# The first query block and the last key block of a macaron attention: from three reduced 32-bit matmuls to one plain 32-bit matmul

## The reference

```python
x = x + 0.5 * ffn(layernorm(x))     # 16 experts of width 128, top 2, plus a shared part of width 512
x = x + attention(layernorm(x))
x = x + 0.5 * ffn(layernorm(x))     # the same weights again
```

```python
qkv = q @ w_qkv.T                                          # 4096 + 1024 + 1024 columns
scores = einsum('bskgd,btkd->bkgst', qh, kh) / sqrt(128)
scores = where(causal, scores, finfo.min)
probs = softmax(scores, axis=-1)
attn = einsum('bkgst,btkd->bskgd', probs, vh)
return attn.reshape(B, S, 4096) @ w_dense.T
```

## Time and profile before

| what | value |
|---|---|
| median of three executions | 1210.75 us |
| profiled execution | 1207.59 us, of which the span is 1205.9 us |
| TensorE matmul busy | 1130.7 us, 94% of the span |
| VectorE, ScalarE, GpSimd busy | 701.6, 557.6 and 473.4 us |
| TensorE's share of the chain that ended last | 86% |
| stretch from 250 to 960 us (attention) | TensorE busy 708.59 of 710 us |

### The profile page before, as it was taken

One profiled execution on the slowest core, in us unless ns is written; L12 is line 12 of the kernel. 1 busy time (PEld: TensorE's weight loads), 2 busy tenths in 40 slices (PEclk: granted clock), 3 DMA queues, 4 the chain that ended last, 5 costly groups with the idle time before them and its releaser, 6 DMA issues.

```text
span 1205.9 us, 20326 instructions
## 1 busy us (share of the span) xinstructions
PE 1130.7 (94%) x6110; PEld 943.2 (78%) x6111; DVE 701.6 (58%) x1836; ACT 557.6 (46%) x1352; POOL 473.4 (39%) x485
## 2 busy tenths in 40 slices
PE   5989996789999999999999999999999989989994
PEld 4777774678888888888888888888888876877773
DVE  5767776855455545454545454554554556867766
ACT  3336662346435445344544443534553543246650
POOL 1266556116315324323432532531532410365545
PEclk9999998889999999999999999999999999999998
DMA  9986547101101010010010110010100007744546
GB/s 356 346 303 212 161 148 244 53 1 36 53 2 36 9 44 0 35 52 0 35 52 0 35 52 0 35 52 0 35 1 1 1 15 287 301 141 157 160 144 209
DMA packets 38603, 114.62 MB, mean 95 GB/s; under 512 B 4384, under 2 KB 4384, under 8 KB 36512
## 3 DMA queue, kind: packets, MB, share of 16 engines
q1 hardware_dynamic: 33440, 97.30, 22.4%
q0 software_dynamic: 5120, 16.78, 4.1%
HBM read 79.20 MB, written 34.87 MB: 95 GB/s over the span
## 4 chain that ended last, share of the span: by engine, by line
PE 86%; DVE 4%; DMA 3%; issue 2%; ACT 2%; POOL 2%; DVEq 0%; SPq 0%; ACTq 0%; POOLq 0%
PE bank L1221 22%; PE bank L1286 15%; PE bank L1252 10%; PE bank L1298 10%; PE bank L1200 7%; PE bank L1127 6%; PE bank L1234 6%; PE bank L1208 4%; PE bank L1143 2%; POOL yg L484 2%; PE bank L1169 2%; PE bank L1188 1%; PE bank L1100 1%; DMA raw_w<-in_ffn_w 1%; PE bank L1088 1%
## 5 line engine op out<-in xcount | busy, mean ns | idle before, releaser
L498 POOL TENSOR_TENSOR scores<-scores,pinv 128x512 f32<-128x512 f32 (+3 forms) x256 | 176.7, 723 | 378.9 <-DVE pinv L996 378.9
L651 ACT ACTIVATE pT_hi<-bank 128x384 fp32r<-128x384 f32 (+1 forms) x192 | 93.9, 524 | 137.1 <-PE bank L1234 137.1
L450 POOL TENSOR_TENSOR tback_lo<-experts,tback_hi 128x768 fp32r<-128x768 f32 x62 | 115.0, 1857 | 74.4 <-ACT tback_hi L593 73.4
L676 ACT ACTIVATE oT_hi<-bank 128x512 fp32r<-128x512 f32 x64 | 38.3, 599 | 221.5 <-PE bank L1298 221.5
L664 ACT ACTIVATE scores<-scores,nmax 128x512 f32<-128x512 f32 (+3 forms) x256 | 140.3, 557 | 0.3 <-DVE nmax L986 0.3
L966 DVE TENSOR_TENSOR pT_lo<-bank,pT_hi 128x384 fp32r<-128x384 f32 (+1 forms) x192 | 109.5, 598 | 46.9 <-ACT pT_hi L651 46.8
L986 DVE CUSTOM_DVE_ANT_0 scores<-bank,causal 128x512 f32<-128x512 f32 (+3 forms) x256 | 112.2, 486 | 2.2 <-issue 0.2
L970 DVE TENSOR_TENSOR oT_lo<-bank,oT_hi 128x512 fp32r<-128x512 f32 x64 | 44.3, 692 | 112.7 <-ACT oT_hi L676 112.7
L1286 PE MATMUL bank<-wds_hi,oT_hi 128*128 128x512 f32 x256 | 105.5, 412 | 1.4 <-DVE oT_lo L970 1.4
L1221 PE MATMUL bank<-xnT_hi,wqs_hi 128*128 128x512 f32 x256 | 106.7, 417 | 0.0
L1221 PE MATMUL bank<-xnT_lo,wqs_hi 128*128 128x512 f32 x256 | 101.8, 398 | 0.0
(11 more groups left out here) (192 smaller groups left out, 2854.0 us busy)
## 6 DMA issues: line engine op xcount, KB each, us to landing
experts<-in_ffn_w SPq DMA_DIRECT2D x32, 768.0 KB, 10.1
xn<-x_rows SPq DMA_DIRECT2D x62, 256.0 KB, 2.7
y_rows<-xn SPq DMA_DIRECT2D x62, 256.0 KB, 2.0
raw_q<-in_wq SPq DMA_DIRECT2D x8, 1024.0 KB, 5.3
raw_d<-in_wd SPq DMA_DIRECT2D x8, 1024.0 KB, 4.8
x_rows<-experts SPq DMA_DIRECT2D x1, 7936.0 KB, 30.0
raw_w<-in_ffn_w SPq DMA_DIRECT2D x8, 768.0 KB, 7.6
raw_kv<-in_wkv SPq DMA_DIRECT2D x8, 512.0 KB, 3.3
```

Of the source, the lines that this page charges most:

```text
L450: nc.gpsimd.tensor_tensor(tback[par][1][:], experts[:, bass.ds(at + FRONT, GU - FRONT)], tback[par][0][:].bitcast(F32), ALU.subtract).then ...
L498: nc.gpsimd.tensor_tensor(s, s, pinv[k % 2][:, i:i + 1].to_broadcast([P, P * (i + 1)]), ALU.mult).then_inc(att.normed, 1)
L651: nc.scalar.activation(pT[0][:, lo_col:hi_col], bank[b][:, 0:hi_col - lo_col], ACT.Copy).then_inc(att.t_hi, 1)
```

## The change

Six plain 32-bit tiles of 128 by 128 are added. ScalarE copies into them, from the same PSUM banks as before: the first 128 queries (`q_first`), the first 128 keys (`k_first`, one for each of two buffers), the last 128 values (`v_last`, two buffers), and the last 128 columns of the transposed probabilities (`pT_last`). TensorE's product for query block 0 is now one matmul of `q_first` with `k_first`, and for key block 3 one matmul of `v_last` with `pT_last`. The halves of what these blocks read are no longer made for `qT` (384 columns in place of 512), `vv` (384) and the third part of `pT` (256 in place of 384). The halves of `kT` are made in full, since the other query blocks read its first 128 keys.

```diff
@@ turned_hi: the third part of pT, and the copies that ScalarE makes
+                    if n == 2:
+                        nc.scalar.activation(pT_last[:], bank[b][:, hi_col - lo_col:hi_col - lo_col + P], ACT.Copy)
                     nc.scalar.activation(pT[0][:, lo_col:hi_col], bank[b][:, 0:hi_col - lo_col],
                                          ACT.Copy).then_inc(att.t_hi, 1)
+
+                def query(src):
+                    nc.scalar.activation(q_first[:], src[:, 0:P], ACT.Copy)
+                    nc.scalar.activation(qT[0][:, P:], src[:, P:], ACT.Copy).then_inc(att.proj_hi, 1)
+
+                def key(b):
+                    nc.scalar.activation(k_first[b][:], bank[0][:, 0:P], ACT.Copy)
+                    nc.scalar.activation(kT[b][0][:], bank[0][:], ACT.Copy).then_inc(att.proj_hi, 1)
+
+                def value(b):
+                    nc.scalar.activation(v_last[b][:], bank[0][:, 3 * P:], ACT.Copy)
+                    nc.scalar.activation(vv[b][0][:, 0:3, :].rearrange("p c d -> p (c d)"), bank[0][:, 0:3 * P],
+                                         ACT.Copy).then_inc(att.proj_hi, 1)
@@ ScalarE's slot
-                        turned_hi(u - 1, 2, COL[2], TRI[ST], 6)
+                        turned_hi(u - 1, 2, COL[2], COL[3], 6)
-                        nc.scalar.activation(qT[0][:], bank[0][:], ACT.Copy).then_inc(att.proj_hi, 1)
+                        query(bank[0])
...
@@ VectorE's slot
-                        turned_lo(u - 1, 2, COL[2], TRI[ST], 6)
+                        turned_lo(u - 1, 2, COL[2], COL[3], 6)
-                        low(qT[1][:], bank[0][:], qT[0][:], att.proj_out)
+                        low(qT[1][:, P:], bank[0][:, P:], qT[0][:, P:], att.proj_out)
...
-                            low(vv[1 - b][1][:].rearrange("p c d -> p (c d)"), bank[0][:],
-                                vv[1 - b][0][:].rearrange("p c d -> p (c d)"), att.proj_out)
+                            low(vv[1 - b][1][:, 0:3, :].rearrange("p c d -> p (c d)"), bank[0][:, 0:3 * P],
+                                vv[1 - b][0][:, 0:3, :].rearrange("p c d -> p (c d)"), att.proj_out)
...
@@ TensorE's slot
                             for i, c in tiles:
+                                if i == 0:
+                                    last = nc.tensor.matmul(bank[bk][:, c:c + P], q_first[:], k_first[b][:],
+                                                            start=True, stop=True)
+                                    continue
                                 for m, (a, z) in enumerate(PARTS):
...
                         for j in range(ST):
                             if j != 3:
                                 pe.wait_ge(att.t_lo, 3 * (u - 1) + j + 1)
+                            if j == ST - 1:
+                                last = nc.tensor.matmul(bank[1][:, j * P:SEQ], v_last[bu][:], pT_last[:],
+                                                        start=False, stop=True, skip_group_check=True)
+                                continue
                             for m, (a, z) in enumerate(PARTS):
```

More of the change, by code:

```diff
@@ L162, in build @@
             causal = sb("causal", [P, 512], F32, st)
+            q_first = sb("q_first", [P, P], F32, st)
+            k_first = [sb(f"k_first{b}", [P, P], F32, st) for b in range(2)]
+            v_last = [sb(f"v_last{b}", [P, D], F32, st) for b in range(2)]
+            pT_last = sb("pT_last", [P, P], F32, st)
             nmax = [sb(f"nmax{p}", [P, ST], F32, st) for p in range(2)]
@@ L683, in slot @@
                         if r == 1:
[L684 removed]
+                            key(1 - b)
                         else:
[L686 to L687 removed]
+                            value(1 - b)
                     if k < 8:
@@ L698, in attention @@
                 turned_norm(1, 0)
-                for n, dst, b in ((1, kT[0][0][:], 0), (3, qT[0][:], 4),
-                                  (4, vv[0][0][:].rearrange("p c d -> p (c d)"), 0)):
-                    act.wait_ge(att.proj_mm, n)
-                    nc.scalar.activation(dst, bank[b][:], ACT.Copy).then_inc(att.proj_hi, 1)
+                act.wait_ge(att.proj_mm, 1)
+                key(0)
+                act.wait_ge(att.proj_mm, 3)
+                query(bank[4])
+                act.wait_ge(att.proj_mm, 4)
+                value(0)
                 att_slots(act, slot)
@@ L1033, in attention @@
                 dve.wait_ge(att.proj_hi, 2)
-                low(qT[1][:], bank[4][:], qT[0][:], att.proj_out)
+                low(qT[1][:, P:], bank[4][:, P:], qT[0][:, P:], att.proj_out)
                 dve.wait_ge(att.proj_hi, 3)
-                low(vv[0][1][:].rearrange("p c d -> p (c d)"), bank[0][:],
-                    vv[0][0][:].rearrange("p c d -> p (c d)"), att.proj_out)
+                low(vv[0][1][:, 0:3, :].rearrange("p c d -> p (c d)"), bank[0][:, 0:3 * P],
+                    vv[0][0][:, 0:3, :].rearrange("p c d -> p (c d)"), att.proj_out)
                 att_slots(dve, slot)
@@ L1299, in slot @@
                                                         pT[z][:, COL[j]:COL[j] + SEQ - j * P],
-                                                        start=(j == 0 and m == 0), stop=(j == ST - 1 and m == 2),
+                                                        start=(j == 0 and m == 0), stop=False,
                                                         skip_group_check=True)
```

3 lines of the change are left out of this document (removed).

## The result

| | before | changed |
|---|---|---|
| median, us (runs, lowest to highest) | 1209.16 (6, 1206.61 to 1211.13) | 1189.81 (6, 1187.85 to 1191.67) |
| profiled execution, us (span) | 1207.59 (1205.9) | 1191.12 (1189.4) |
| mean granted clock in it | 0.984 | 0.982 |

The changed kernel is faster: the ratio of the times is 0.9842 with the interval 0.9822 to 0.9861, 19.1 us by the ratio. Two more comparisons, each on a chip of its own, gave 0.9877 (0.9855 to 0.9899) and 0.9868 (0.9847 to 0.9889). The mean of the three is 0.9862, or 16.6 us, and the two profiled executions differ by 16.5 us. The forecast was 14.2 us and 1195.0; the median lies just under the range's low end of 1190.5.

A forecast was written before the change was run, and what follows sets the result against it. TensorE was taken to bound the attention. 14.5 us saved less 0.3 gives 14.2 off the profiled 1207.59, so 1193.4; half of 3.2 us added for a median of runs gives 1195.0, range 1190.5 to 1200.

The forecast's parts named there:

- Steps 1 and 2: On TensorE, three reduced 128-column matmuls cost 0.34 us together; one plain 32-bit matmul of 128 columns costs 0.222 us.
- Step 3: On TensorE, two places in each of 64 units save 0.113 us each, 14.5 us over 128 places.
- Steps 4 and 5: ScalarE's added copies, net 0.14 us a slot, hide in idle time; VectorE's shorter halves save about 0.3 us a slot.
- Step 6: Bank 0's hand-over after the keys' projection: margin before the next query's projection shrinks from 1.08 to 0.8 us, no new wait.
- Step 7: At the attention's end, TensorE waits longer for `pT_lo`, which takes 0.3 us off the saving.
- A: At the plain matmuls, each change of kind exposes half or all of a 0.11 us pass: 1202 or 1208 us; chance 0.07.
- B: Each of 128 plain matmuls costs four passes, 0.444 us, so 14 us more, 1223 us; chance 0.03.
- C: ScalarE's copies delay TensorE in every slot, by over 0.8 us; at 1.03 us the time is about 1209; chance 0.03.
- Two of the signs: In the changed profile: first pass to next matmul about 0.22 us; stages around the attention change by at most 1 us.

The follow-up runs named there:

- twice: The changed kernel with the scores' plain matmul issued twice, writing the same scores again; 1206.05 us, ratio to the kernel before 0.9994.
- scores_only: The kernel before with only the scores of the first 128 queries as one plain matmul, the values' product as before; 1200.41 us, ratio 0.9941.
- values_only: The kernel before with only the product with the last 128 keys as one plain matmul, the scores as before; 1199.71 us, ratio 0.9939.
- side_only: The kernel before with its matmuls kept, but the change's plain copies and shorter halves on ScalarE and VectorE in units 8 to 55; 1205.82 us, ratio 0.9995.
- after_pad: The changed kernel with one unread reduced 128-column matmul added behind the scores' plain one; 1201.85 us, ratio 0.9927.
- third_after: The changed kernel run a third time, with no edit; 1190.23 us, ratio 0.9868.
- act_more: The changed kernel with three more unread ScalarE copies ahead of `pT_last` in each slot and six ahead of `k_first`; 1201.67 us, ratio 0.9926.
- two_parts: The kernel before without one of the three reduced matmuls of the first query block's scores; 1207.84 us, ratio 0.9972.
- before_fill: The kernel before with 20 unread reduced 512-column matmuls in TensorE's waits of units 0 and 1; 1206.55 us, ratio 1.0003.

## Why the prediction was right in its mechanism and short in its sum

- **What bounds the kernel: right.** TensorE is busy for 99.8% of the attention's middle part before and 99.6% after, it has no wait between 262 and 960 us in either, and what its instructions lose is lost by the kernel.
- **Steps 1 and 2: right.** Three reduced matmuls of 128 columns were 0.34 us; the plain one costs 0.222, and twice measured 0.223 for one more. Reading two records in the earlier trace rows as two passes decided the sign.
- **Step 3: the step that failed, by a term that it put at nothing.** For its two places it holds: 0.219 us a unit against 0.226. But the unit is 0.250 us shorter. All but 0.002 of the missing 0.031 us is on the 512-column matmuls of the query's projection and the output product, 0.029 us a unit and 1.9 us in all. The step counted only instructions that the change touches, and gave no reason why the others should keep their length. The runs show that the term comes with the scores' plain matmul (scores_only has it, values_only and side_only have not), and goes, in whole or in part, when the scores are made long again (twice, after_pad).
- **Steps 4 and 5: right in the main.** side_only: ratio 0.9995, no steady unit changed. Step 5 also said that the first units' waits for `qT_lo` and `pT_lo` get no longer. The one for `qT_lo` went from 1.9 to 2.2 us in the profiled executions (1.8 in third_after), and that of line 1234 for `pT_lo` from 2.3 to 2.4.
- **Step 6: right.** 0.79 us left against 0.8, and act_more found the edge where copies use it up.
- **Step 7: right in sign, and too large.** It took 0.3 us off for a longer wait for `pT_lo`, which grew by 0.1.
- **The rivals fell.** A by the 0.219 us of the two places, changes of kind included; B by 0.223 for a whole plain matmul; C by side_only.
- **Two of the signs read otherwise.** The first matmul behind the passes starts 0.14 us after the first pass and not 0.22, because its record starts early; the count to the second one holds. And the prediction called itself wrong if the stages ahead of or behind the attention changed by more than 1 us. In the profiled executions they did, by 3.4 us more and 1.4 less, but the stage ahead differs as much between executions of one kernel: unit 0's scores start at 229.1 to 233.3 us in the changed kernel's three profiles. So this sign was too narrow to judge the change by.

Measured by the unit, the sum is 64 x 0.25 - 0.1 = 15.9 us and not 14.2: 14.0 from the two places, 1.9 beside them, 0.1 in small differences, less 0.1 of wait. The profiled executions differ by 16.5 and the comparisons by 16.6 on the mean. The 15.9 still lies in the forecast of 12 to 16, so the rest of the miss is in how the range was placed. It stood on three executions of the kernel before, the lowest of them (1207.58) taken as the fast end, while executions of that kernel went down to 1202.3 and its median lay between 1206.55 and 1210.94 in different comparisons. In the three comparisons in which the changed kernel ran, 37 executions of the kernel before have the mean 1207.6 us; 15.9 less is 1191.7. The 16 executions of the changed kernel have the mean 1190.75, and half of them lie under 1190.5. The low end of the range therefore stood in the middle of the changed kernel's times, and that the first six had their median 0.7 us below it and not above is chance. The agreement in the profiles is partly luck too: the 16.5 us contain a gain of 3.2 and a loss of 3.4 us that the change did not make.

What stays open: why the 512-column matmuls beside the scores take a step of 0.015 to 0.02 us less in most units. after_pad shows that it goes with the length of the scores; two_parts, and the one unit in four of scores_only that keeps its old lengths, show that this is not all.

## What to carry to other kernels

A narrow reduced matmul is not cheap by its columns: at 128 columns it cost 0.113 us and at 256 columns 0.12, while a plain 32-bit one cost two passes of 0.111, so one plain matmul in place of three reduced ones pays at the narrow tile. At 512 columns, by the rows, it would cost 0.86 us in place of 0.7. Price such an edit by distances between starts, over many repeats, and measure what the untouched neighbours do too: here they made an eighth of the saving. Before a range is set, ask how far executions of the unchanged program lie apart, and how much of that the granted clock explains.

## What the runs showed of the hardware

- A plain 32-bit matmul is two records. At 128 columns each is 0.111 us, at 512 columns 0.43; a pass therefore costs by its columns down to 128, while a reduced matmul stops getting cheaper at 256 (0.23, 0.12 and 0.113 us for 512, 256 and 128 columns).
- The distance between starts of 512-column reduced matmuls with nothing waiting is not constant. Twelve of them took 2825 to 2850 ns on the mean as the output product and 2881 to 2899 as the query's projection, depending on instructions elsewhere in the unit. In single units the output product took 2.820, 2.838 or 2.854 us, each within 0.002, and nothing between; the means are the same to 1 ns in each repeat of a kernel. The projections of keys and of values took 2.852 us behind three reduced 128-column matmuls and 2.878 behind the plain one.
- The granted clock fell to half for stretches of 3.4 to 17.1 us. The longest lie in and behind TensorE's wait of 12.4 us ahead of the first projection, and behind the waits of the first units, but which stretches there are and how long differs between executions of one kernel. At the halved clock the start distance of 512-column reduced matmuls is 0.43 instead of 0.23 us. Executions of one kernel lay up to 10 us apart within one comparison, and the time goes only loosely with the mean granted clock. Fillers that kept TensorE busy in one such place (before_fill) kept the clock full there, and the time of the kernel was the same.
